# Making the adjacency masks of graphs 2 to 15 on GpSimd instead of VectorE, and waiting for the stored output later

## The chip, the core and the metric

The kernel runs on one core of a Trainium2 chip. A core has five engines that run in parallel, each through its own list of instructions in order, and that wait for each other with semaphores: TensorE (PE; its weight loads are listed as PEld), VectorE (DVE), ScalarE (ACT), GpSimd (POOL) and SyncE (SP), which here only issues DMAs. SBUF is the memory on chip that all of them read and write, PSUM the one that TensorE writes its products to. The metric is the device time of one launch in microseconds (us).

## What is computed

There are 16 graphs of 512 nodes with 256 features. Each goes through two layers of one-head attention and then one layer of eight-head attention, all under the mask that its adjacency matrix gives. Cut to what matters:

```python
mask = adj == 0                                    # adj: (16, 512, 512) int32
for k in range(2):                                 # layers L, of one head
    q = x @ Wq[k].T + bq[k];  kk = x @ Wk[k].T + bk[k]
    scores = where(mask, -1e10, q @ kk.T / SCALE)
    attn = where(mask, 0.0, softmax(scores, axis=2))
    x = layer_norm(x + (attn @ x) @ Wc[k].T, ln_g[k], ln_b[k])
q, k, v = (x @ W + b, split into 8 heads of 32)    # layer H
scores = where(mask, -inf, q @ k.T / sqrt(32))
h = softmax(scores, axis=-1) @ v
out = layer_norm(h @ Wo + bo + x, gamma, beta)
```

## The kernel before

**Tiles and slots.** A tile is 128 rows of one 512x512 score matrix. For each tile TensorE multiplies the scores into a PSUM bank (`ps_s`, three banks), VectorE scales them, adds the mask and takes the row minimum (`masked_s`, line 1017), ScalarE takes the exponential (`probs`, L928), TensorE transposes the result (`ps_t`, L789), and ScalarE copies it to SBUF, or VectorE does for every fourth tile (L934, L1024). Four tiles are a slot: one head (H) of a graph or one layer (L) of it. TensorE makes scores four tiles ahead of the tile that it transposes, and VectorE masks three tiles ahead. With three banks, the scores of tile k+3 need the masking of tile k to be done.

**Loop.** After a prologue, 14 rounds of ten slots (`LOOP_SLOTS`, 40 tiles) run, then a tail. Round i handles heads of graphs i and i+1 and the two one-head layers of graph i+2. The table `LOOP_JOBS` says behind which of the 40 tiles each of the other pieces of work is put, in the lists of all engines that share in it. The names used below: AV is the weighted sum of a one-head layer, N the normalisation of its result `y_l` on VectorE (L1118, it needs `rstd_L` from GpSimd), QK and XW the projections of a one-head layer (`qt`, `kt`, `xw`), QH and V those of the eight-head layer, OG the head outputs, R a reciprocal (L1128), WO the output projection, and M the making of a mask.

**Masks.** Graph b's adjacency comes in two halves of 2 x 128 rows. Both go through the same buffer, `adj_t`, so SyncE issues the load of half 1 (`load_adj`, L449) only when the mask of half 0 has been made. VectorE makes the mask with one instruction for each half, on 128 partitions x 1024 elements, int32 in and bf16 out: (adj == 0) * MASKED (L1069). Half 0 is at `LOOP_JOBS` position 0, half 1 at position 5. The result `mask_a0` serves layer 0 of the graph, and DMAs copy it to `mask_a1` and `mask_h` for the later layers.

**GpSimd's list.** In each round GpSimd copies the residual (`residual`, L677), and then handles two layer norms (`layer_norm_l0`: L622 `rstd_L`, L635 and L637 the split of `y_l` into two fp16 parts `ys`, L627 gain, L629 shift), one split of the next input, and at the end `finish` for graph i: `rstd_F`, four scalings (L684), gain, shift, and the DMA that stores the output (L690). `finish` ends with a wait for that DMA to have landed (`out_stored`), since the residual copy that follows overwrites the same `y_f`.

**The split `ys`** is turned by a DMA transpose (L497) into `xt2`, from which TensorE makes QH some tiles later.

Of the kernel before, what the change touches and what calls it, by code (L numbers as in the profile page):

```python
# [9 lines left out]
NT = N // P  # L10
# [4 lines left out]
MASKED = -1e33  # L15
# [7 lines left out]
LOOPS = NB - 2  # L23
# [7 lines left out]
LOOP_JOBS = [  # L31
    ("AV", (1, 2), "i+1", 1, (0, 0, 1, 1)),
    ("N", None, "i+1", 1, (4,)),
    ("M", None, "i+2", 0, (0,)),
    ("OG", (1, 0), "i", 0, (3, 5, 7)),
    ("R", None, "i", 0, (3,)),
    ("M", None, "i+2", 1, (5,)),
    ("QK", (0, 2), "i+2", 0, (2, 4)),
    ("XW", (2, 0), "i+2", 0, (8, 10)),
    ("QH", (1, 2), "i+1", 0, (12, 13)),  # L40
# [63 lines left out]
def graph_attention(nc, x, adj, l0, l1, out):  # L104
    fp32, fp16, bf16, i32 = mybir.dt.float32, mybir.dt.float16, mybir.dt.bfloat16, mybir.dt.int32
    ALU, ACT = mybir.AluOpType, mybir.ActivationFunctionType
# [6 lines left out]
    with ctx:  # L113
        def sb(name, shape, dt=fp32):
            return ctx.enter_context(nc.sbuf_tensor(name, shape, dt))

        def sem(name):
            return ctx.enter_context(nc.semaphore(name))
# [29 lines left out]
        mask_a0 = sb("mask_a0", [P, NT, N], bf16)  # L148
# [68 lines left out]
        mask0_ready, mask1_ready = sem("mask0_ready"), sem("mask1_ready")  # L217
        maskh_ready = [sem(f"maskh{r}_ready") for r in range(NT)]
        scores_done, masked, exps = sem("scores_done"), sem("masked"), sem("exps")
# [27 lines left out]
        xres_ready, out_stored = sem("xres_ready"), sem("out_stored")  # L247
# [14 lines left out]
        def slots_before(i):  # L262

            return sum(len(slots) for _, slots, _, _ in PRO_BLOCKS) + len(LOOP_SLOTS) * i
# [3 lines left out]
        def nth(b, l):  # L268

            if isinstance(b, int) and b + l == 1:  # L270
                return 2 if l else 1
            return 2 * b + l
# [36 lines left out]
        def x_loaded(b):  # L309

            if early(b, 2):
                return (x_in, 16) if b == 0 else (x1_in, 16)
            return x_in, 16 * b

        def adj_tile(b, h):

            if early(b, 2):
                return (adj_t[:], adj_spare)[h] if b == 0 else adj_next[:, 2 * h:2 * h + 2]
            return adj_t[:]

        def adj_loaded(b, h):

            if early(b, 2):
                return (adj_in, 32) if b == 0 else (adj1_in, 32)
            return adj_in, 16 * (2 * b + h - 1)

        def early(count, n):

            return isinstance(count, int) and count < n

        def settle(eng):


            eng.sem_inc(waits_passed, 1)
# [275 lines left out]
        @blk.gpsimd  # L610
        def _(pool):
            pool.memset(ident[:], 1.0).then_inc(ident_zero, 1)
            pool.memset(minus_half[:], -0.5).then_inc(half_in, 1)
            pool.memset(mean_64[:], 1.0 / 64).then_inc(mean_in, 1)
            pool.wait_ge(ident_zero, 1)
            pool.affine_select(out=ident[:], in_=ident[:], compare_op=ALU.is_equal, fill=0.0, base=0,
                               pattern=[[-1, P]], channel_multiplier=1).then_inc(ident_in, 1)

            def rstd_of(s, c):

                pool.wait_ge(moments_ready[s], c + 1)
                pool.tensor_tensor(rstd[s][:], var_eps[s][:], minus_half[:], ALU.pow).then_inc(rstd_ready[s], 1)  # L622

            def gain_and_shift(s, c, y, norm, dst):
                g = gain[:, norm:norm + 1, :].to_broadcast([P, NT, D])
                h = shift[:, norm:norm + 1, :].to_broadcast([P, NT, D])
                pool.tensor_tensor(dst[:], y[:], g, ALU.mult).then_inc(gained[s], 1)  # L627
                pool.wait_ge(gained[s], c + 1)
                pool.tensor_tensor(dst[:], dst[:], h, ALU.add).then_inc(ln_done[s], 1)  # L629

            def split(src, dst, high, ready, n):


                src = src[:].rearrange("p t (c k) -> p c t k", c=DC)
                pool.tensor_copy(dst[:, 0], src).then_inc(high, 1)  # L635
                pool.wait_ge(high, n + 1)
                pool.tensor_tensor(dst[:, 1], src, dst[:, 0], ALU.subtract).then_inc(ready, 1)  # L637

            def split_x(b):

                pool.wait_ge(*x_loaded(b))
                settle(pool)
                if not early(b, 1):
                    pool.wait_ge(xt_in, 16 * (nth(b - 1, 0) + 1))
                    settle(pool)
                split(x_tile(b), xs, xs_hi, xs_ready, b)

            def split_y(b, l):
                rstd_of("L", nth(b, l))

                pool.wait_ge(normed["L"], nth(b, l) + 1)
                settle(pool)

                if l == 0 and early(b, 2):
                    if b == 1:
                        pool.wait_ge(xt_in, 16 * (nth(0, 1) + 1))
                        settle(pool)
                elif l == 1 and early(b, 1):
                    pool.wait_ge(xt_in, 16 * (nth(1, 1) + 1))
                    settle(pool)  # L660
                else:
                    pool.wait_ge(xt2_in, 16 * b)
                    settle(pool)
                    if l == 1:
                        pool.wait_ge(xt_in, 16 * (nth(b, 1) + 1))
                        settle(pool)
                split(y_l, ys, ys_hi, ys_ready, nth(b, l))

            def layer_norm_l0(b, l, dst):
                split_y(b, l)  # L670
                gain_and_shift("L", nth(b, l), y_l, l, dst)

            def residual(b):

                pool.wait_ge(ln_done["L"], 2 * NB if isinstance(b, int) and b == NB - 1 else 2 * b + 3)
                settle(pool)
                pool.tensor_copy(y_f[:], x2[:]).then_inc(xres_ready, 1)  # L677

            def finish(b):
                rstd_of("F", b)  # L680
                pool.wait_ge(rstd_ready["F"], b + 1)
                settle(pool)
                for t in range(NT):
                    last = pool.tensor_scalar(y_f[:, t], y_f[:, t], minus_mean["F"][:, t:t + 1],  # L684
                                              rstd["F"][:, t:t + 1], ALU.add, ALU.mult)
                last.then_inc(normed["F"], 1)
                pool.wait_ge(normed["F"], b + 1)
                gain_and_shift("F", b, y_f, 2, y_f)
                pool.wait_ge(ln_done["F"], b + 1)
                pool.dma_start(out_v[b], y_f[:]).then_inc(out_stored, 16)  # L690
                pool.wait_ge(out_stored, 16 * (b + 1))

            split_x(0)
            split_x(1)
            pool.wait_ge(weights_in, 16 * N_WEIGHTS_IN)

            pool.tensor_tensor(shift[:, 1], shift[:, 1], bo1, ALU.add).then_inc(bo_added, 1)
            pool.wait_ge(bo_added, 1)
            layer_norm_l0(0, 0, x1)

            split_y(1, 0)
            pool.tensor_tensor(y_f[:], y_l[:], gain[:, 0:1, :].to_broadcast([P, NT, D]), ALU.mult)\
                .then_inc(gained["L"], 1)
            split_x(2)
            pool.wait_ge(y_ready["L"], 2 * nth(0, 1) + 2)
            settle(pool)
            pool.wait_ge(gained["L"], nth(1, 0) + 1)
            pool.tensor_tensor(x1[:], y_f[:], shift[:, 0:1, :].to_broadcast([P, NT, D]), ALU.add)\
                .then_inc(ln_done["L"], 1)
            layer_norm_l0(0, 1, x2)  # L710
            for i in range(LOOPS - 1):
                residual(i)
                layer_norm_l0(i + 1, 1, x2)
                layer_norm_l0(i + 2, 0, x1)
                split_x(i + 3)
                finish(i)
            residual(LOOPS - 1)
            layer_norm_l0(LOOPS, 1, x2)
            layer_norm_l0(LOOPS + 1, 0, x1)
            finish(LOOPS - 1)  # L720
            residual(NB - 2)
            layer_norm_l0(NB - 1, 1, x2)
            finish(NB - 2)
            residual(NB - 1)
            rstd_of("F", NB - 1)
# [275 lines left out]
        def _(dve):  # L1001
# [58 lines left out]

            def make_mask(b, h):

                if h == 0 and not early(b, 1):
                    dve.wait_ge(mask1_ready, 16 * b)
                if early(b, 2) and b == 1:
                    dve.wait_ge(masked, NT)
                dve.wait_ge(*adj_loaded(b, h))
                settle(dve)
                dve.tensor_scalar(mask_a0[:, 2 * h:2 * h + 2], adj_tile(b, h), 0.0, MASKED, ALU.is_equal,  # L1069
                                  ALU.mult).then_inc(mask0_ready, 1)  # L1070
# [194 lines left out]
```

## Time and profile before

| | us |
|---|---|
| median of the three runs shown | 1263.99 |
| lowest, highest | 1263.12, 1269.35 |
| the profiled execution, its own time | 1263.8 |
| its span in the profile | 1262.1 |
| busy: PE, DVE, ACT, POOL | 1168.8, 1046.9, 879.6, 491.5 |
| granted TensorE clock | 0.994 of full speed |

The span is the time from the first to the last recorded instruction; the launch takes 1.7 us more. Each engine's busy time is the time in which it had an instruction in execution. The profile and the trace come from one execution, so every duration below is of that one.

### The profile page before, as it was taken

What the parts mean: (1) busy time and instruction counts of PE and PEld (TensorE: products, weight loads), DVE (VectorE), ACT (ScalarE), POOL (GpSimd) and SP (SyncE); (2) the same over time, 40 slices, a digit from 0 to 9 for tenths busy, and PEclk for the clock granted to TensorE, in tenths of its full rate; (3) what the DMA queues carried; (4) which work ended last, traced back from release to release, by engine and by line L of the source; (5) the groups of instructions that cost most, each with busy time, mean ns of one, the idle gap of its engine ahead of it and who ended that gap; (6) DMA issues with size and microseconds to landing.
All of it is one profiled execution on the core that took longest, in us unless ns stands there. A gap on an engine that the chain in (4) does not pass through costs nothing.

```text
span 1262.1 us, 28364 instructions
## 1 busy us (share of the span) xinstructions
PE 1168.8 (93%) x9440; PEld 843.7 (67%) x9440; DVE 1046.9 (83%) x2771; ACT 879.6 (70%) x2018; POOL 491.5 (39%) x338
## 2 busy tenths in 40 slices
PE   4876999999999999999999999999999999999896
PEld 2643667677676767767676776767677676776564
DVE  3776888979798897979889797988979888897786
ACT  3235786777778677786767778676777867677674
POOL 2342233443363344336333433633344354334420
PEclk9999999999999999999999999999999999999999
DMA  8115263353625234271523527254342724333321
GB/s 251 50 34 137 48 159 76 103 117 92 160 51 163 73 101 118 83 169 51 153 84 100 118 71 182 52 136 100 97 122 69 183 52 138 97 81 89 84 69 34
DMA packets 182208, 130.84 MB, mean 104 GB/s; under 512 B 108464, under 2 KB 161712, under 8 KB 182064
## 3 DMA queue, kind: packets, MB, share of 16 engines
q1 hardware_dynamic: 179904, 121.16, 37.3%
q0 software_dynamic: 2160, 7.87, 1.8%
q8 instruction: 78, 1.28, 0.4%
q14 instruction: 66, 0.54, 0.1%
HBM read 61.87 MB, written 25.17 MB: 69 GB/s over the span
## 4 chain that ended last, share of the span: by engine, by line
PE 52%; DVE 23%; issue 11%; ACT 10%; DMA 2%; SPq 1%; POOL 1%; DVEq 0%; ACTq 0%; POOLq 0%
PE ps_j L776 17%; PE ps_t L789 13%; PE ps_j L877 9%; DVE masked_s L1017 8%; PE ps_s L768 5%; ACT probs L928 4%; PE ps_j L894 4%; PE ps_s L762 3%; DVE y_l L1161 2%; ACT pt_h L934 2%; DVE pt_l L1052 2%; DVE parts L1169 2%; DVE stats_L L1037 2%; ACT parts L973 1%; ACT xw L965 1%
## 5 line engine op out<-in xcount | busy, mean ns | idle before, releaser
L928 ACT ACTIVATE probs<-masked_s,nm_h 128x512 f32<-128x512 f32 x512 | 367.7, 718 | 137.6 <-DVE nm_h L1017 136.5
L789 PE MATMUL ps_t<-ident,probs 128*128 128x128 f32 x2560 | 390.6, 275 | 37.7 <-ACT pt_h L934 20.1
L789 PEld LDWEIGHTS ps_t<-ident,probs 128*128 128x128 f32 x2560 | 301.6, 141 | 132.7 <-ACT probs L928 63.6
L1017 DVE CUSTOM_DVE_ANT_0 masked_s<-ps_s,mask_h 128x512 f32<-128x512 f32 x512 | 341.9, 681 | 54.8 <-PE ps_s L768 54.6
L934 ACT ACTIVATE pt_h<-ps_t 128x512 f32<-128x512 f32 x376 | 221.9, 590 | 93.6 <-PE ps_t L789 90.2
L768 PE MATMUL ps_s<-stack 128*128 128x512 f16 x512 | 194.0, 380 | 9.2 <-DVE nm_h L1017 6.5
L776 PE MATMUL ps_j<-xw,pt_l 128*128 128x256 f16 x1536 | 186.3, 276 | 3.6 <-DVE pt_l L1052 3.6
L776 PEld LDWEIGHTS ps_j<-xw,pt_l 128*128 128x128 f16 x1536 | 151.9, 99 | 32.4 <-DVE pt_l L1052 3.9
L622 POOL TENSOR_TENSOR rstd_L<-var_eps_L,minus_half 128x4 f32<-128x4 f32 x32 | 32.8, 1024 | 301.3 <-DVE var_eps_L L1047 301.3
L877 PE MATMUL ps_j<-pt_h,v 128*32 128x256 f32 x2048 | 123.6, 382 | 1.7 <-DVE pt_h L1024 1.7
L622 POOL TENSOR_TENSOR rstd_F<-var_eps_F,minus_half 128x4 f32<-128x4 f32 x16 | 16.3, 1018 | 275.5 <-DVE var_eps_F L1047 275.5
L776 PE MATMUL ps_j<-xt,wq 128*128 128x512 f16 x384 | 95.7, 386 | 20.1 <-DMA xt<-xs 13.6
L1024 DVE COPY pt_h<-ps_t 128x512 f32<-128x512 f32 x136 | 93.3, 686 | 19.0 <-PE ps_t L789 18.7
L1052 DVE TENSOR_TENSOR pt_l<-ps_t,pt_l 128x512 f16<-128x512 f32 x128 | 88.3, 690 | 19.5 <-ACT pt_l L934 13.4
L928 ACT ACTIVATE probs<-masked_s,nm_l 128x512 f32<-128x512 f32 x128 | 92.1, 720 | 16.2 <-DVE nm_l L1017 16.2
L776 PE MATMUL ps_j<-wc,xt 128*128 128x256 f16 x768 | 97.8, 273 | 5.0 <-DVE qt L1136 5.0
L934 ACT ACTIVATE pt_l<-ps_t 128x512 f16<-128x512 f32 x96 | 56.7, 591 | 62.8 <-PE ps_t L789 62.7
L762 PE MATMUL ps_s<-kt,qt 128*128 128x512 f16 x372 | 99.6, 379 | 0.2
L928 ACT ACTIVATION_READ_ACCUMULATOR probs<-masked_s,nm_h 128x1 f32 x512 | 97.8, 191 | 0.0
L877 PEld LDWEIGHTS ps_j<-pt_h,v 128*32 128x32 f32 x2048 | 60.3, 109 | 53.2 <-issue 19.3
L776 PE MATMUL ps_j<-xt,wk 128*128 128x512 f16 x384 | 94.0, 381 | 0.0
L776 PEld LDWEIGHTS ps_j<-wc,xt 128*128 128x128 f16 x768 | 74.9, 98 | 25.7 <-issue 5.8
(107 smaller groups left out, 1718.9 us busy)
## 6 DMA issues: line engine op xcount, KB each, us to landing
stack<-bounce SPq DMA_DIRECT2D x256, 128.0 KB, 3.2
bounce<-parts SPq DMA_DIRECT2D x64, 256.0 KB, 3.1
adj_t<-adj_dram SPq DMA_DIRECT2D x29, 512.0 KB, 4.7
x<-x_dram SPq DMA_DIRECT2D x16, 512.0 KB, 4.0
mask_a<-mask_a SPq DMA_DIRECT2D x16, 512.0 KB, 4.0
mask_h<-mask_a SPq DMA_DIRECT2D x64, 128.0 KB, 3.3
out_dram<-y_f POOLq DMA_DIRECT2D x15, 512.0 KB, 3.4
stack<-adj_dram SPq DMA_DIRECT2D x2, 512.0 KB, 5.8
```

Source lines behind the costliest of these rows:

```text
L622: pool.tensor_tensor(rstd[s][:], var_eps[s][:], minus_half[:], ALU.pow).then_inc(rstd_ready[s], 1)
L762: last = pe.matmul(dst, q_t[:, a, r * P:(r + 1) * P], k_t[:, c], start=n_ == 0, stop=n_ == 2)
L768: pe.matmul(dst, stack[:, n, 0, r * P:(r + 1) * P], stack[:, n, 1, :], start=True, stop=True).then_inc(scores_done, 1)
L776: last = pe.matmul(dst, lhs(a, e), rhs(c, e), start=n == 0, stop=n == len(terms) - 1 and not more)
L789: last = pe.transpose(ps_t[r % 2][:, t], probs[:, r, t * P:(t + 1) * P], ident[:])
L877: last = pe.matmul(out_bank[h * HD:(h + 1) * HD, 2 * r * P:2 * (r + 1) * P], v1[:, t, col:col + HD], pt_h[:, h, t, 2 * r * P:2 * (r + 1) * P],
L894: last = pe.matmul(out_bank[:, t * D:(t + 1) * D], ot[:, g, at:at + P], wo1[:, g], start=g == 0, stop=g == 1)
L928: act.activation(probs[:, r], masked_s[:, r], ACT.Exp, bias=nm[:, n, r:r + 1], scale=-1.0, accum_out=total[:, n, r:r + 1]).then_inc(exps, 1)
L934: act.activation(dst, ps_t[r % 2][:], ACT.Copy).then_inc(copied_act, 1)
L1017: dve.tensor_tensor_reduce(out=masked_s[:, r], in0=ps_s[scores_bank(pos)][:], in1=m[:, r], scale=-scale, scalar=NONE_LEFT, op0=ALU.add, op ...
L1024: dve.tensor_copy(dst, ps_t[r % 2][:]).then_inc(copied_dve, 1)
L1052: dve.tensor_tensor(dst, full, high, ALU.subtract).then_inc(ready, 1)
```

## The change

The two M entries leave the table of the loop, so VectorE makes masks only for graphs 0 and 1, in the prologue. GpSimd gets a `make_mask` of its own, with the same instruction. It calls it for half 0 ahead of the residual copy of a round, and for half 1 behind that copy and ahead of the layer norm that was next. The wait for the stored output leaves the end of `finish` and stands at the start of the next `residual`, so behind mask half 0.

```diff
@@ LOOP_JOBS
-    ("M", None, "i+2", 0, (0,)),
     ("OG", (1, 0), "i", 0, (3, 5, 7)),
     ("R", None, "i", 0, (3,)),
-    ("M", None, "i+2", 1, (5,)),
@@ gpsimd
+            def make_mask(b, h, passed):
+
+                if h == 0:
+                    pool.wait_ge(mask1_ready, 16 * b)
+                    settle(pool)
+                    pool.wait_ge(masked, passed)
+                    settle(pool)
+                pool.wait_ge(*adj_loaded(b, h))
+                settle(pool)
+                pool.tensor_scalar(mask_a0[:, 2 * h:2 * h + 2], adj_tile(b, h), 0.0, MASKED, ALU.is_equal,
+                                   ALU.mult).then_inc(mask0_ready, 1)
+
             def residual(b):
 
+                if not early(b, 1):
+                    pool.wait_ge(out_stored, 16 * b)
+                    settle(pool)
                 pool.wait_ge(ln_done["L"], 2 * NB if isinstance(b, int) and b == NB - 1 else 2 * b + 3)
@@ finish
                 pool.dma_start(out_v[b], y_f[:]).then_inc(out_stored, 16)
-                pool.wait_ge(out_stored, 16 * (b + 1))
@@ the rounds
             for i in range(LOOPS - 1):
+                make_mask(i + 2, 0, NT * slots_before(i))
                 residual(i)
+                make_mask(i + 2, 1, NT * slots_before(i))
                 layer_norm_l0(i + 1, 1, x2)
                 layer_norm_l0(i + 2, 0, x1)
                 split_x(i + 3)
                 finish(i)
+            make_mask(LOOPS + 1, 0, NT * slots_before(LOOPS - 1))
             residual(LOOPS - 1)
+            make_mask(LOOPS + 1, 1, NT * slots_before(LOOPS - 1))
             layer_norm_l0(LOOPS, 1, x2)
@@ vector
             def make_mask(b, h):
 
-                if h == 0 and not early(b, 1):
-                    dve.wait_ge(mask1_ready, 16 * b)
-                if early(b, 2) and b == 1:
+                if b == 1:
                     dve.wait_ge(masked, NT)
```

GpSimd's list where round 0 ends and round 1 begins, before (`x` and `y_f` are the residual's source and target):

```order
L629 TENSOR_TENSOR y_f<-y_f,shift 128x1024 [waits gained_F]
L690 DMA out_dram<-y_f 128x4x256 [waits ln_done_F]
L677 COPY y_f<-x 128x1024 [waits out_stored,ln_done_L]
L622 TENSOR_TENSOR rstd_L<-var_eps_L,minus_half 128x4 [waits moments_ready_L]
L635 CAST ys<-y_l 128x1024 [waits normed_L,xt2_in,xt_in]
L637 TENSOR_TENSOR ys<-y_l,ys 128x1024 [waits ys_hi]
```

and now:

```order
L627 TENSOR_TENSOR y_f<-y_f,shift 128x1024 [waits gained_F]
L703 DMA out_dram<-y_f 128x4x256 [waits ln_done_F]
L680 TENSOR_SCALAR mask_a<-adj_t 128x1024 [waits mask1_ready,masked,adj_in]
L690 COPY y_f<-x 128x1024 [waits out_stored,ln_done_L]
L680 TENSOR_SCALAR mask_a<-adj_t 128x1024 [waits adj_in]
L620 TENSOR_TENSOR rstd_L<-var_eps_L,minus_half 128x4 [waits moments_ready_L]
L633 CAST ys<-y_l 128x1024 [waits normed_L,xt2_in,xt_in]
```

The two masks stand around the copy, both of them ahead of `rstd_L`.

VectorE's list around mask half 1 in the same round, before (`y_l` L1118 is N, `kt` the low part of the QK projection, the two ISA rows of L1017 the masking of one tile and the reading of its row minimum):

```order
L1017 ISA masked_s,nm_h<-ps_s,mask_h 128x512 [waits scores_done,exps]
L1017 ISA nm_h 128x1
L1118 TENSOR_SCALAR y_l<-y_l,minus_mean_L,rstd_L 128x256 [waits rstd_ready_L]
L1118 TENSOR_SCALAR y_l<-y_l,minus_mean_L,rstd_L 128x256 x3
L1136 SCALAR_TENSOR_TENSOR kt<-ps_j,bk,kt 128x512 [waits qk_hi]
L1017 ISA masked_s,nm_h<-ps_s,mask_h 128x512 [waits scores_done,exps]
L1017 ISA nm_h 128x1
L1069 TENSOR_SCALAR mask_a<-adj_t 128x1024 [waits adj_in]
L1017 ISA masked_s,nm_h<-ps_s,mask_h 128x512 [waits scores_done,exps]
L1017 ISA nm_h 128x1
L1024 COPY pt_h<-ps_t 128x4x128 [waits transposed]
```

and now:

```order
L1033 ISA masked_s,nm_h<-ps_s,mask_h 128x512 [waits scores_done,exps]
L1033 ISA nm_h 128x1
L1132 TENSOR_SCALAR y_l<-y_l,minus_mean_L,rstd_L 128x256 [waits rstd_ready_L]
L1132 TENSOR_SCALAR y_l<-y_l,minus_mean_L,rstd_L 128x256 x3
L1150 SCALAR_TENSOR_TENSOR kt<-ps_j,bk,kt 128x512 [waits qk_hi]
L1033 ISA masked_s,nm_h<-ps_s,mask_h 128x512 [waits scores_done,exps]
L1033 ISA nm_h 128x1
L1033 ISA masked_s,nm_h<-ps_s,mask_h 128x512 [waits scores_done,exps]
L1033 ISA nm_h 128x1
L1040 COPY pt_h<-ps_t 128x4x128 [waits transposed]
```

Only the mask row is gone. Half 0 leaves in the same way, further up in the same round. The lists of TensorE, ScalarE and SyncE are the same in both kernels.

## Rows read from the trace of the kernel before

**Rows 1.** The page, part 1: busy time, share of the span, instructions.

```profile
PE 1168.8 (93%) x9440; PEld 843.7 (67%) x9440; DVE 1046.9 (83%) x2771; ACT 879.6 (70%) x2018; POOL 491.5 (39%) x338
```

**Rows 2.** Busy time by engine in one stretch of 74 us, then clock, DMA share.

```profile
358.00:432.00 74.00, 71.73 (x590) 52.42 (x588) 63.94 (x170) 54.91 (x127) 31.12 (x21) 1.00 0.40 108
```

**Rows 3.** Busy time of line 1069 alone, from the first round to the last.

```profile
137.00:1115.00 978.00, 39.54 (x28) 1.00 0.42 107
```

**Rows 4.** TensorE, 425 to 472 us: start, length, line, work, idle before and releaser.

```profile
427.11 0.63 PE L789 MATMUL ps_t<-ident,probs 128*128 128x128 f32 x4 [0.83 <-DVE pt_l L1052]
...
445.09 0.81 PE L762 MATMUL ps_s<-kt,qt 128*128 128x512 f16 x3
...
452.27 1.46 PE L776 MATMUL ps_j<-xt,wq 128*128 128x512 f16 x6
453.56 0.60 PE L789 MATMUL ps_t<-ident,probs 128*128 128x128 f32 x4
...
470.04 0.39 PE L768 MATMUL ps_s<-stack 128*128 128x512 f16 x1 [0.46 <-DVE nm_h L1017]
471.45 0.63 PE L789 MATMUL ps_t<-ident,probs 128*128 128x128 f32 x4 [1.03 <-ACT pt_h L934]
```

**Rows 5.** VectorE, 432 to 446 us, same columns.

```profile
432.74 0.68 DVE L1069 TENSOR_SCALAR mask_a<-adj_t 128x1024 bf16<-128x1024 int32 x1
...
439.34 0.69 DVE L1017 CUSTOM_DVE_ANT_0 masked_s<-ps_s,mask_h 128x512 f32<-128x512 f32 x1 [0.26 <-PE ps_s L768]
...
439.95 1.38 DVE L1118 TENSOR_SCALAR y_l<-y_l,minus_mean_L,rstd_L 128x256 f32<-128x256 f32 x4
442.10 0.75 DVE L1136 SCALAR_TENSOR_TENSOR kt<-ps_j,bk,kt 128x512 f16<-128x512 f32 x1 [0.77 <-ACT kt L962]
442.77 0.68 DVE L1017 CUSTOM_DVE_ANT_0 masked_s<-ps_s,mask_h 128x512 f32<-128x512 f32 x1
...
443.37 2.13 DVE L1069 TENSOR_SCALAR mask_a<-adj_t 128x1024 bf16<-128x1024 int32 x1
```

**Rows 6.** GpSimd, 430 to 447 us, same columns.

```profile
430.79 0.83 POOL L690 DMA_DIRECT2D out_dram<-y_f  x1 [0.30 <-POOL y_f L629]
434.40 1.03 POOL L677 COPY y_f<-x 128x1024 f32<-128x1024 f32 x1 [2.77 <-DMA out_dram<-y_f]
436.48 1.03 POOL L622 TENSOR_TENSOR rstd_L<-var_eps_L,minus_half 128x4 f32<-128x4 f32 x1 [1.06 <-DVE var_eps_L L1047]
441.69 1.04 POOL L635 CAST ys<-y_l 128x1024 f16<-128x1024 f32 x1 [4.18 <-DVE y_l L1118]
442.81 2.14 POOL L637 TENSOR_TENSOR ys<-y_l,ys 128x1024 f16<-128x1024 f32 x1
```

**Rows 7.** SyncE's issues, 430 to 450 us, same columns.

```profile
433.51 0.40 SPq L449 DMA_DIRECT2D adj_t<-adj_dram  x1
445.18 1.74 SPq L497 DMA_TRANSPOSE xt<-ys  x1
```

**Rows 8.** That load's time from issue to landing: round at 507, then at 432 us.

```profile
adj_t<-adj_dram SPq DMA_DIRECT2D x1, 512.0 KB, 3.6
...
adj_t<-adj_dram SPq DMA_DIRECT2D x1, 512.0 KB, 5.0
```

**Rows 9.** Landing of the transposes by line 497, all 16: least, median, most.

```profile
DMA to landing us min/median/max: 4.2/4.3/5.9
```

**Rows 10.** GpSimd's groups: busy us, mean ns of one, idle before them.

```profile
L684 POOL TENSOR_SCALAR y_f<-y_f,minus_mean_F,rstd_F 128x256 f32<-128x256 f32 x60 | 32.5, 551 | 3.2 <-POOL rstd_F L622 3.2
L616 POOL TENSOR_SCALAR_AFFINE_SELECT ident<-ident 128x128 f32<-128x128 f32 x1 | 0.3, 284 | 0.0
```

**Rows 11.** ScalarE and VectorE, 453 to 456 us: how the next busy run of VectorE begins.

```profile
453.63 0.72 ACT L928 ACTIVATE probs<-masked_s,nm_l 128x512 f32<-128x512 f32 x1 [0.18 <-DVE nm_l L1017]
...
454.35 0.58 ACT L934 ACTIVATE pt_l<-ps_t 128x512 f16<-128x512 f32 x1
...
455.04 0.69 DVE L1052 TENSOR_TENSOR pt_l<-ps_t,pt_l 128x512 f16<-128x512 f32 x1 [0.18 <-ACT pt_l L934]
```

## The prediction

> **What bounds the kernel now.** The page's busy times come first [rows 1]: TensorE works 93% of the span, VectorE 83%, GpSimd 39%. Read by stage, the rounds are tighter still: of 74 us in one round TensorE is busy 71.73 [rows 2], so only 2.27 us in a round are open to any change that leaves TensorE's own work alone, 14 x 2.27 = 32 us in all. The next question is where in the round these 2.27 us lie. TensorE's timeline shows idle time in two places only: before 427.11 (0.83 us), and before 470.04 and 471.45 (0.46 and 1.03 us), the rest being crumbs [rows 4]. Each time the releaser is VectorE or ScalarE behind it. Between 427.7 and 469 TensorE's instructions follow each other without a wait. Both masks of the round, at 432.74 and 443.37 [rows 5], lie in that stretch. So VectorE's time there isn't what the round's length is made of.
>
> **What is removed.** 28 mask instructions leave VectorE, with 39.54 us together [rows 3], 2.8 us in a round: 0.68 us for half 0, 2.13 us for half 1 [rows 5]. It is the same instruction; the second starts at 443.37 while GpSimd's subtraction of `ys` runs from 442.81 to 444.95 [rows 6], and 444.95 + 0.55 is the 445.50 at which it ends. What the 39.54 us are worth on the path: in the stretch of the masks TensorE has no wait to lose, so nothing there. Of the gain something gets through only if VectorE enters its next full stretch earlier, the one at whose end the two idle times at 470 and 471 lie. That stretch begins at 455.04 with a statement that waited 0.18 us for ScalarE's copy of 454.35, which came late because ScalarE's exponential had waited 0.18 us for a masking at 453.63 [rows 11]. The copy can't start before its transposes, 453.56 with 0.60 us [rows 4], are through at 454.16 and have been signalled. So an earlier VectorE moves the start of the full stretch by 454.35 - 454.2 = 0.15 us, no more. 13 to 14 rounds x 0.15 = 2 us faster.
>
> The Trainium skill, "SBUF — State Buffer", section "Who interferes with whom", says that VectorE's two-port instructions and GpSimd's hold the shared ports exclusively, and that the later one blocks in full. The 2.13 us against 0.68 agree with it. By that rule alone 1.45 us of each round's 2.8 was blocking and would be gained too; by the timeline it is hidden like the rest.
>
> **What is added: GpSimd's two masks.** Their length D has no row. The nearest from below is a one-input copy of the same 1024 elements, 1.03 us [rows 6]. From above: the scaling with two operations takes 0.551 us for 256 elements, four of which are 2.2; the one instruction with a comparison, 0.284 us for 128, would give 8 x 0.284 = 2.3 [rows 10]. Fixed costs are counted four and eight times in these, so the value lies between the ends; I take D = 1.8, and keep 1.0 to 2.3 as likely, with more as a rival.
>
> The Trainium skill, "GPSIMD Engine Reference", section "Engine selection", says that one-input operations on GpSimd run at roughly line rate. The copy's row agrees, the scaling's row does not, and the mask is of the scaling's kind. With D = 1.0 by the page the sum below would be the same 2 us.
>
> **Half 0** costs nothing: the DMA issue ends at 430.79 + 0.83 = 431.6, and GpSimd then waited 2.77 us, to 434.40, for the stored output [rows 6]. The mask fills that wait (431.7 to 433.5 with D = 1.8), which is what moving `out_stored` behind it allows. Its other conditions are met: VectorE's own mask at 432.74 started without a wait for the adjacency [rows 5], and VectorE masks three tiles ahead, so the round's last tile is masked well before its end. The cover is gone at D above 2.7.
>
> **Half 1** is the dear one, since it stands ahead of `rstd_L`, on which VectorE's N waits with everything behind it. With L the landing time of the load: half 0 ends at 431.7 + D, SyncE issues 0.1 later (433.51 after 433.42 before), the data are there L later, the mask takes D, `rstd_L` 1.03 and the semaphores between 0.25. N can start at 431.8 + D + L + D + 1.3 = 433.1 + L + 2D. It started at 439.95, right after a masking that TensorE had held [rows 5], so the missing half 0 mask doesn't bring it forward. The delay is S = L + 2D - 6.85. L is 3.6 us in the round at 507 and 5.0 in the one at 432 [rows 8]; of the 14 rounds nine are within 0.1 us of the first value, and the other five go up to the second. With D = 1.8 S is 0.35 us with the short load and 1.75 with the long one.
>
> Who waits for that? Behind N stand `kt` and the masking of 442.77 [rows 5]. TensorE needs both at 445.09 [rows 4] (`kt` directly, and the masking because it frees the bank). From N's start the three take 1.33 + 0.67 + 0.68 = 2.7 us (1.38, 0.75, 0.68 in their rows, of which the first two overlap the next a little), and must be done by 445.0: N may start at 442.3, so S may be 2.35. After that masking VectorE saves the 2.13 us of half 1, so every later statement is earlier than before. The other follower is the split `ys`, which moves with N; its transpose was issued at 445.18 [rows 7] and lands 4.3 us later [rows 9], at 449.5, and TensorE's QH begins at 452.27 [rows 4]: 2.8 us of slack. Both hold for S = 1.75. Half 1's cost: 0, as long as L + 2D < 9.2, that is D < 2.8 with the short load and D < 2.1 with the long one. At the upper end, D = 2.3, three or four rounds with the long load lose 0.4 us, less than 2 us in all. The prologue and the tail keep their lists.
>
> **The sum.** 1263.8 (the profiled run) - 2 + 0 = 1261.8; against the median 1263.99 it is the same within 0.2 us. I forecast 1262.
>
> **The rivals.**
>
> *GpSimd's mask is slow, and half 1 holds VectorE (slower).* For: no row shows a comparison on 1024 int32 elements, and GpSimd's power of 4 elements takes 1.03 us [rows 6], so some operations there are far from the copy's rate. It decides from D = 2.8. Beyond it each of 13 rounds loses S - 2.35 = L + 2D - 9.2, with L = 4.0 on average 2D - 5.2: at D = 3.0 0.8 us, 10 us together and 1272; at D = 4.0 2.8 us, 36 us and 1298. Against: the three nearest rows give 1.0 to 2.3. Chance 0.18, most of it near the threshold, with the price at D = 3.0 as its own forecast.
>
> *VectorE's relief comes through (faster).* VectorE has 2.8 us less in each round, and if its backlog instead of the order of arrival makes the idle times at 470 and 471, they close: 14 x 1.49 = 21 us, 1243; a third of it is 1257. For: VectorE is the releaser, and runs without idle time before it. Against: it waits for ScalarE at 455.04 [rows 11], between the masks and that stretch, so that the gained time is given back there. Chance 0.12.
>
> *The change doesn't fill a wait.* Half 1 is not in the 2.77 us but in the 4.18 us that GpSimd waited for N [rows 6], which itself waits for what GpSimd has to do first. This is the first rival at smaller D, and costs nothing below the threshold; its chance of 0.1 is inside that of no change.
>
> **How the numbers follow.** What a measurement of this kernel can tell from no change is about 0.5%, 6.3 us. Hidden, as summed: 0.70. Slower: 0.18. Faster: 0.12. The forecast's own spread is 1258 to 1268. The range goes down to 1253, past the third of the relief, and up to 1275, past the D = 3.0 case; outside remain some 0.08 on the slow side and 0.07 on the fast side.
>
> **What would show it.** VectorE's busy time falls by about 39 us and GpSimd's rises by 28 x D, near 50. `out_dram`'s wait before the residual copy shrinks from 2.77 us to about 0.9. GpSimd's idle time before half 1 is charged to the load `adj_t`. VectorE gets a wait of 0.3 to 1.8 us on `rstd_L` before N in each round, and TensorE has none in that stretch. Its idle times at 427, 470 and 471 stay, the last two shorter by 0.15. A mask longer than 2.8 us on GpSimd, or an idle TensorE before the scores that use `kt`, would make the forecast wrong upward; the idle time at 470 gone would make it wrong downward.

## The result and the profile after

| | before | after |
|---|---|---|
| median, four runs each | 1265.77 | 1286.32 |
| lowest, highest | 1263.12, 1269.35 | 1283.1, 1288.03 |
| the profiled execution, and its span | 1263.8, 1262.1 | 1286.17, 1284.4 |

The changed kernel is slower: the ratio is 1.0158, with a 95% interval of 1.0122 to 1.0193. The forecast was 1262 us, 2 us below the kernel before, with a range of 1253 to 1275. The measured time lies above the range, and the change went the other way.

Part 1 of the page of after, which answers to [rows 1], gives busy time, share of the span and instructions:

```profile
PE 1181.2 (92%) x9440; PEld 850.0 (66%) x9440; DVE 1012.7 (79%) x2743; ACT 882.4 (69%) x2018; POOL 586.4 (46%) x366
```

VectorE lost 34 us of work and GpSimd gained 95, on a span that is 22.3 us longer. What GpSimd gained is named by its groups (part 5 of the page: busy us, mean ns of one, idle time before them and what ended it):

```profile
L680 POOL TENSOR_SCALAR mask_a<-adj_t 128x1024 bf16<-128x1024 int32 x28 | 102.2, 3650 | 68.9 <-DMA adj_t<-adj_dram 41.9 <-DVE nm_h L1033 26.5
```

One mask takes 3.65 us on GpSimd. The forecast had put 1.8 on it, from rows of 1.0 to 2.3 us [rows 10].

The round at 511 us shows what this does. First GpSimd, 505 to 535 us (start, length, line, work, idle before and releaser), which answers to [rows 6]:

```profile
510.14 0.87 POOL L703 DMA_DIRECT2D out_dram<-y_f  x1 [0.30 <-POOL y_f L627]
511.05 3.67 POOL L680 TENSOR_SCALAR mask_a<-adj_t 128x1024 bf16<-128x1024 int32 x1
514.66 1.04 POOL L690 COPY y_f<-x 128x1024 f32<-128x1024 f32 x1
518.77 3.63 POOL L680 TENSOR_SCALAR mask_a<-adj_t 128x1024 bf16<-128x1024 int32 x1 [3.06 <-DMA adj_t<-adj_dram]
522.37 1.04 POOL L620 TENSOR_TENSOR rstd_L<-var_eps_L,minus_half 128x4 f32<-128x4 f32 x1
525.19 1.04 POOL L633 CAST ys<-y_l 128x1024 f16<-128x1024 f32 x1 [1.78 <-DVE y_l L1132]
```

SyncE issues the load of half 1 behind the first mask, and it lands 3.8 us later (SyncE's timeline, and the DMA issues of that stretch, which answer to [rows 7] and [rows 8]):

```profile
514.83 0.40 SPq L447 DMA_DIRECT2D adj_t<-adj_dram  x1
```

```profile
adj_t<-adj_dram SPq DMA_DIRECT2D x1, 512.0 KB, 3.8
```

VectorE in the same round, which answers to [rows 5]:

```profile
515.72 0.16 DVE L1063 TENSOR_SCALAR var_eps_L<-moments_L 128x4 f32<-128x4 f32 x1
...
518.86 0.69 DVE L1033 CUSTOM_DVE_ANT_0 masked_s<-ps_s,mask_h 128x512 f32<-128x512 f32 x1 [0.30 <-PE ps_s L784]
...
523.44 1.38 DVE L1132 TENSOR_SCALAR y_l<-y_l,minus_mean_L,rstd_L 128x256 f32<-128x256 f32 x4 [3.88 <-POOL rstd_L L620]
524.74 0.75 DVE L1150 SCALAR_TENSOR_TENSOR kt<-ps_j,bk,kt 128x512 f16<-128x512 f32 x1
525.40 0.68 DVE L1033 CUSTOM_DVE_ANT_0 masked_s<-ps_s,mask_h 128x512 f32<-128x512 f32 x1
```

And TensorE, which answers to [rows 4]:

```profile
524.19 0.60 PE L805 MATMUL ps_t<-ident,probs 128*128 128x128 f32 x4
526.15 0.82 PE L778 MATMUL ps_s<-kt,qt 128*128 128x512 f16 x3 [1.36 <-DVE nm_h L1033]
```

Read the four together. The input of `rstd_L`, `var_eps_L`, is there at 515.9 us. But `rstd_L` stands in GpSimd's list behind mask half 1, whose data land at 518.6, so it starts at 522.37. N on VectorE waits 3.88 us for it. The masking behind N therefore ends at 526.1, and TensorE, whose next scores need that bank and `kt`, stands still for 1.36 us. Before, the scores that use `kt` began without a wait, in the round at 432 us [rows 4] as in the one at 507 us, which is the round shown here:

```profile
519.35 0.81 PE L762 MATMUL ps_s<-kt,qt 128*128 128x512 f16 x3
```

How often TensorE waits like this is in the views of waits of after, over the whole span (waiting line, released by: us in total, times, longest). TensorE:

```profile
PE ps_s L778 <- DVE nm_h L1033: 16.7, 13, 1.6
```

GpSimd and VectorE:

```profile
POOL mask_a L680 <- DMA adj_t<-adj_dram: 41.9, 14, 3.1
```

```profile
DVE y_l L1132 <- POOL rstd_L L620: 52.4, 17, 4.1
```

So 16.7 of the 22.3 us are this wait, 13 times, 0.8 to 1.6 us each. Of the rest, 3.4 us are in the tail, where the one long wait for a transpose of `ys` is 3.18 us (2.35 before) and the granted clock then drops. In the windows of after (us, busy time and instructions of PE, PEld, DVE, ACT, POOL, then clock, DMA share, GB/s) it is 0.83 over 20 us, where the same work before had 1.00 throughout:

```profile
1205.00:1215.00 10.00, 8.74 (x41) 5.00 (x42) 3.85 (x11) 4.80 (x10) 0.62 (x1) 0.83 0.10 37
1215.00:1225.00 10.00, 7.81 (x44) 5.46 (x42) 7.20 (x20) 9.52 (x25) 0.00 (x0) 0.83 0.79 227
```

Another 1.7 us are in two late rounds, in which TensorE waits 0.61 and 0.42 us for a transpose of `ys`. That transpose comes later because N does: it is issued 2.5 us behind the start of the scores that use `kt` in almost every round, against 0.1 us before. In these two rounds it also landed late, 5.4 and 5.2 us after its issue where 4.3 is usual. Such a landing alone did no harm before (5.9 us in two rounds, no wait), and the later issue alone does none in the others; the two together use up the 2.8 us of slack that the prediction had found. Round 0 is a control inside the run: there GpSimd had its first mask made by 131.8, half 1 started at 135.81, N at 144.08 waited for nothing, and TensorE had no such wait.

### The profile page after: what moved, and what is told of

It is laid out like the page before. It is cut to its first block, busy times and chain, and to the rows that moved or that the text cites. A ratio compares the mean times of both kernels' runs of the same rounds, so it can differ in the third digit from the quotient of the medians.

```text
span 1284.4 us, 28406 instructions
## 1 busy us (share of the span) xinstructions
PE 1181.2 (92%) x9440; PEld 850.0 (66%) x9440; DVE 1012.7 (79%) x2743; ACT 882.4 (69%) x2018; POOL 586.4 (46%) x366
## 3 DMA queue, kind: packets, MB, share of 16 engines
q8 instruction: 78, 1.28, 0.4%
## 4 chain that ended last, share of the span: by engine, by line
PE 41%; DVE 21%; POOL 17%; issue 8%; DMA 6%; ACT 6%; SPq 1%; DVEq 0%; POOLq 0%; ACTq 0%
PE ps_j L792 12%; PE ps_t L805 11%; POOL mask_a L680 7%; PE ps_j L893 6%; DVE masked_s L1033 5%; PE ps_s L778 5%; PE ps_j L910 4%; DMA adj_t<-adj_dram 3%; PE ps_s L784 3%; ACT probs L944 2%; POOL y_f L625 2%; POOL y_f L627 2%; DVE y_l L1175 2%; POOL y_f L697 2%; DVE parts L1183 2%
## 5 line engine op out<-in xcount | busy, mean ns | idle before, releaser
L805 PEld LDWEIGHTS ps_t<-ident,probs 128*128 128x128 f32 x2560 | 305.0, 142 | 130.2 <-ACT probs L944 59.8
L680 POOL TENSOR_SCALAR mask_a<-adj_t 128x1024 bf16<-128x1024 int32 x28 | 102.2, 3650 | 68.9 <-DMA adj_t<-adj_dram 41.9
L778 PE MATMUL ps_s<-kt,qt 128*128 128x512 f16 x372 | 100.3, 382 | 16.8 <-DVE nm_h L1033 16.7
L792 PE MATMUL ps_j<-xt,wk 128*128 128x512 f16 x384 | 96.9, 390 | 0.0
```

What stands on the lines that cost most here:

```text
L680: pool.tensor_scalar(mask_a0[:, 2 * h:2 * h + 2], adj_tile(b, h), 0.0, MASKED, ALU.is_equal, ALU.mult).then_inc(mask0_ready, 1)
L778: last = pe.matmul(dst, q_t[:, a, r * P:(r + 1) * P], k_t[:, c], start=n_ == 0, stop=n_ == 2)
L792: last = pe.matmul(dst, lhs(a, e), rhs(c, e), start=n == 0, stop=n == len(terms) - 1 and not more)
L805: last = pe.transpose(ps_t[r % 2][:, t], probs[:, r, t * P:(t + 1) * P], ident[:])
```

## The experiments

Theory **A**: the mask of 3.65 us, twice in a chain with the load between them and ahead of `rstd_L`, holds N. Rival **B**: GpSimd's longer work gets in the way of VectorE's by itself, wherever it stands. Rival **C**: it is the later wait for the stored output. Each median below stands beside that of the kernel before on the same chip, over 10 runs of the experiment's kernel where nothing else is said. The ratio on record, with its 95% interval, isn't the quotient of the two medians and can differ from it by 0.1%; the verdicts go by the ratio.

**1. Mask half 1 behind the split of `ys`.** Same masks, same lengths; only `rstd_L` and the split go first. This tells A from B.

```diff
-            def layer_norm_l0(b, l, dst):
+            def layer_norm_l0(b, l, dst, masks=None):
                 split_y(b, l)
+                if masks is not None:
+                    make_mask(masks, 1, 0)
...
-                make_mask(i + 2, 1, NT * slots_before(i))
-                layer_norm_l0(i + 1, 1, x2)
+                layer_norm_l0(i + 1, 1, x2, masks=i + 2)
...
```

> The changed kernel with one thing moved: GpSimd makes mask half 1 behind the split of y_l into ys, no longer ahead of rstd_L. Theory A (VectorE's N waits for rstd_L behind mask half 1, 3.65 us each, and TensorE then waits 1.2 to 1.5 us a round for the masking behind N): the 3.9 us wait before N and TensorE's wait go, 1264 +-3. Theory B (GpSimd's 102 us of masks slow the other engines wherever they run, by the shared port or by memory): the masks are still there, so about the changed kernel's time, 1283 to 1289. Theory C (half 1 here ends too late for the first use of the mask, some 3.7 us behind): about 1270, with a wait of VectorE on the mask.

Measured: 1263.65 beside 1265.86, ratio 0.9988 (0.9972 to 1.0004). The whole loss is gone. GpSimd's timeline of this kernel:

```profile
510.17 1.04 POOL L620 TENSOR_TENSOR rstd_L<-var_eps_L,minus_half 128x4 f32<-128x4 f32 x1 [0.27 <-DVE var_eps_L L1063]
...
518.65 3.65 POOL L682 TENSOR_SCALAR mask_a<-adj_t 128x1024 bf16<-128x1024 int32 x1
```

The mask is as long as ever, so B falls. (The theory C of this expectation isn't the rival C above; it says that half 1 comes too late for its first use.) VectorE now waits for the mask itself, a few tiles later, and its waits of the whole span say so:

```profile
DVE masked_s L1033 <- POOL mask_a L682: 21.7, 14, 1.9
```

In the rounds TensorE has no wait behind that (the scores that use `kt` wait nowhere), so the expectation's theory C costs nothing either. A wait of VectorE costs time only where it outlasts what TensorE can spare behind it.

**2 and 3. One half alone.** Half 0 goes back to VectorE (2, with its old wait for `mask1_ready`), or half 1 does (3).

```diff
@@ 2
+    ("M", None, "i+2", 0, (0,)),
...
-                make_mask(i + 2, 0, NT * slots_before(i))
                 residual(i)
...
@@ 3
+    ("M", None, "i+2", 1, (5,)),
...
                 residual(i)
-                make_mask(i + 2, 1, NT * slots_before(i))
...
```

> Half 0 back on VectorE, half 1 on GpSimd where the change has it. Theory A: the load for half 1 starts when VectorE's half 0 is done, not 3.7 us after GpSimd's DMA issue; N can start at 433.4 + 3.6 + 3.65 + 1.3 = 442.0 by the clock of the round shown of before, 2.1 us late, under the 2.35 us that TensorE tolerates: VectorE waits 2 us for rstd_L in each round, TensorE waits not at all, 1264 +-4. Theory B: half of GpSimd's masks, half of the loss, about 1275.

> Half 0 on GpSimd where the change has it, half 1 back on VectorE. Theory A: half 0 (3.65 us) ends 1 us after the stored output has landed, the residual copy is 1 us late and rstd_L hardly; the load of half 1 lands some 4 us before VectorE's half 1: 1264 +-3. Theory B: half of the loss, about 1275.

Measured: half 1 alone 1270.53 beside 1265.86, ratio 1.0026 (1.001 to 1.0041); half 0 alone 1265.56, ratio 0.9995 (0.9982 to 1.0008). With half 1 alone, D counts once. In the round of an ordinary load N waits 2.10 us:

```profile
517.94 1.38 DVE L1133 TENSOR_SCALAR y_l<-y_l,minus_mean_L,rstd_L 128x256 f32<-128x256 f32 x4 [2.10 <-POOL rstd_L L621]
```

TensorE stands still only in the four rounds with a slow load (its waits, 300 to 1100 us):

```profile
PE ps_s L777 <- DVE nm_h L1032: 3.4, 4, 1.5
```

The forecast for 2 was 1264 +-4 with no wait of TensorE, and the median is 2.5 us above that. It had counted on the short load. In the four rounds that wait, the load took 4.2 to 5.6 us, in the others 3.6 to 3.8. This is the threshold of the prediction, met from both sides. The two halves aren't additive: alone they cost 3 us (5 by the medians) and 0 us, together 20. What half 0 adds is a later load of half 1. SyncE issues it 3.82 us behind the end of GpSimd's DMA issue in the changed kernel (514.83 against 511.01) and 2.05 us behind it in 2 (509.35 against 507.30). The difference of 1.77 us is that of N's waits, 3.88 against 2.10.

**4. The same values by add and multiply.** The adjacency is 0 or 1, so (adj - 1) * (-MASKED) gives the same mask.

```diff
-                pool.tensor_scalar(mask_a0[:, 2 * h:2 * h + 2], adj_tile(b, h), 0.0, MASKED, ALU.is_equal,
+                pool.tensor_scalar(mask_a0[:, 2 * h:2 * h + 2], adj_tile(b, h), -1.0, -MASKED, ALU.add,
```

> The changed kernel with the mask computed as (adj - 1) * 1e33, the same values for an adjacency of 0 and 1, so add and multiply in place of comparison and multiply; same sizes, types and places. If the comparison makes the 3.65 us, the mask takes what the scalings of 4 x 256 elements suggest, about 2.2 us, N can start 2.9 us earlier, which is more than TensorE's wait of 1.3: 1264 +-4. If the 1024 int32 elements make it, 3.6 us and 1286. In between each us of the mask's length is worth 2 us a round down to the threshold, so at 3.0 us the loss is gone.

Measured: 1267.1 beside 1265.86, ratio 0.9999 (0.9985 to 1.0012). The loss is gone here too, with the list of the changed kernel untouched. The mask's line in this kernel (ns: least, median, most), and then in the changed one:

```profile
L680 POOL TENSOR_SCALAR mask_a<-adj_t x28: 1045/1046/1059, 127.6 to 1100.7; 128x1024 bf16<-128x1024 int32 x28
```

```profile
L680 POOL TENSOR_SCALAR mask_a<-adj_t x28: 3627/3644/3685, 128.1 to 1122.9; 128x1024 bf16<-128x1024 int32 x28
```

The same tile, types and number of operations: it is the comparison that costs 2.6 us. The length was expected at 2.2 us and is half of that.

**5. Mask half 1 made twice.** The longer chain, on the other side of the threshold.

```diff
...
+                if h == 1:
+                    pool.tensor_scalar(mask_h2[:], adj_tile(b, h), 0.0, MASKED, ALU.is_equal, ALU.mult)
                 pool.tensor_scalar(mask_a0[:, 2 * h:2 * h + 2], adj_tile(b, h), 0.0, MASKED, ALU.is_equal,
```

> The changed kernel, with GpSimd computing mask half 1 twice in a row (first into a spare buffer), so 3.63 us more between the load and rstd_L in each round. Theory A, TensorE waiting 1:1 for what is behind N: 13 rounds x 3.63 = 47 us on top of the changed kernel, 1333 +-6, and VectorE's wait before N 7.5 us. If something else makes the loss and N's wait only accompanies it, the time rises by less than half of that, under 1310.

Measured, two runs: 1362.22 beside 1266.38, ratio 1.0758 (1.0736 to 1.0779). The direction is A's, but the size is a miss: 76 us over the changed kernel instead of 47. TensorE in one round:

```profile
554.64 1.46 PE L781 MATMUL ps_s<-kt,qt 128*128 128x512 f16 x3 [4.91 <-DVE nm_h L1036]
...
560.69 0.81 PE L781 MATMUL ps_s<-kt,qt 128*128 128x512 f16 x3
```

The wait grew from 1.36 to 4.91 us, by 3.55, as the added 3.6 us ask for. But the three matmuls behind it take 1.46 us and not 0.81. The windows (columns as above) show why:

```profile
555.00:560.00 5.00, 5.00 (x21) 3.27 (x20) 2.70 (x8) 3.25 (x9) 4.92 (x3) 0.51 0.29 56
560.00:565.00 5.00, 5.00 (x36) 3.63 (x35) 3.62 (x8) 4.54 (x11) 1.68 (x1) 1.00 0.27 50
```

TensorE stood still for 4.9 us, and in the 5 us behind that wait it was granted 0.51 of full speed, the lower of its two levels, so it did some 2.4 us less work in them. From the first of these waits to the last the rounds take 81.3 us on average, against 75.5 in the changed kernel. Of these 5.8 us the waits make 3.6 (4.88 against 1.28 on average), and 2.2 are left for the low clock, which every one of the 13 rounds had. 13 x 5.8 is the 76 us.

**6. A buffer of its own for half 1.** The load of half 1 no longer waits for mask half 0; the masks keep their length and place.

```diff
...
+        adj_u = sb("adj_u", [P, NT // 2, N], i32)
...
-            return adj_t[:]
+            return (adj_t, adj_u)[h][:]
...
-            return adj_in, 16 * (2 * b + h - 1)
+            return (adj_u_in, 16 * (b - 1)) if h else (adj_in, 16 * (b + 1))
...
-                    sp.wait_ge(mask0_ready, 2 * b + h)
+                    sp.wait_ge(mask0_ready, 2 * b)
```

> The changed kernel with a second adjacency buffer, so that the load of half 1 no longer waits for mask half 0: the 3 us of the load leave the chain, both masks keep their 3.65 us and their places. Theory A: from the start of half 0 to N there are 3.65 + 1.04 + 3.65 + 1.3 = 9.6 us instead of 12.4; TensorE tolerates 11.0 (12.4 less its wait of 1.36), so it doesn't wait, 1264 +-4, with about 1 us of wait left on VectorE before N. If the masks' own length ahead of rstd_L were enough for the loss, 1275 or more.

Measured: 1266.56 beside 1266.38, ratio 1.0004 (0.9993 to 1.0015). GpSimd, then VectorE, in one round (its first mask starts at 507.12):

```profile
511.75 3.63 POOL L682 TENSOR_SCALAR mask_a<-adj_u 128x1024 bf16<-128x1024 int32 x1
```

```profile
516.42 1.38 DVE L1134 TENSOR_SCALAR y_l<-y_l,minus_mean_L,rstd_L 128x256 f32<-128x256 f32 x4 [0.34 <-POOL rstd_L L622]
```

N starts 9.3 us after the first mask instead of 12.4, inside what TensorE tolerates, and the scores that use `kt` wait in no round. VectorE's wait before N is 0.34 us, where about 1 us was expected. So the loss has three conditions, and taking any one away is enough: the mask's length (4), the load in series between the masks (6), and the place ahead of `rstd_L` (1).

**7. The moved wait alone.** The kernel before, with `out_stored` waited for at the next residual.

```diff
+                if not early(b, 1):
+                    pool.wait_ge(out_stored, 16 * b)
+                    settle(pool)
...
-                pool.wait_ge(out_stored, 16 * (b + 1))
```

> The kernel before with only the wait for the stored output moved to the start of the next residual copy; the masks stay on VectorE. Nothing stands between the old and the new place of the wait in the rounds, so nothing can change but where it is booked: 1264 +-3, the same as before. If the moved wait had a part in the loss, it is slower.

Measured: 1265.63 beside 1265.8, ratio 1.0005 (0.9991 to 1.002). C falls.

**8 to 11. Is VectorE's time worth anything?** With the loss gone, kernels 1, 4 and 6 still give nothing for the work that VectorE no longer has. The prediction's faster rival said that the idle times at 470 and 471 are VectorE's backlog. So in 8 the layer-0 N, which lies right in VectorE's full stretch, goes from the kernel before to GpSimd, and in 9 from kernel 4:

```diff
-    ("N", None, "i+2", 0, (18,)),
...
+                    for t in range(NT):
+                        last = pool.tensor_scalar(y_l[:, t], y_l[:, t], minus_mean["L"][:, t:t + 1],
+                                                  rstd["L"][:, t:t + 1], ALU.add, ALU.mult)
```

> The kernel before, masks on VectorE as there, but the normalisation of layer 0 (N, four instructions, 1.35 us of VectorE in the full stretch that ends at TensorE's idle times at 470 and 471) done by GpSimd, which sits idle there. If the stretch in which VectorE is full sets those idle times (0.46 + 1.03 us), taking 1.35 us out of it shortens every round by 1.2 to 1.4 us: 1246 to 1250. If ScalarE or the transposes set them, nothing: 1262 to 1266. It tells whether VectorE's time is worth anything, and where.

> The changed kernel with the add and multiply mask (1.05 us) and with layer 0's normalisation on GpSimd. If VectorE's masks are hidden before as the timeline says, this is the same as the normalisation alone on the kernel before, within 0.3%: the masks add nothing to it, 1244 to 1250.

Measured: 8 gives 1266.09 beside 1266.38, ratio 1.0001 (0.9985 to 1.0016), which is the expectation's second branch, nothing gained. 9 gives 1265.12, ratio 0.9991 (0.9978 to 1.0004): the same as 8, as expected, but not the 1244 to 1250. The two idle times of 0.46 and 1.03 us became one of the same sum (TensorE of 8):

```profile
472.62 0.63 PE L795 MATMUL ps_t<-ident,probs 128*128 128x128 f32 x4 [1.50 <-ACT pt_h L940]
```

Its releaser is ScalarE, which has two copies of the QH projection ahead of the exponential and the copy that TensorE waits for (ScalarE of 8, same stretch):

```profile
470.03 0.68 ACT L979 ACTIVATE parts<-ps_j,bq 128x512 f16<-128x512 f32 x1
...
471.17 0.73 ACT L934 ACTIVATE probs<-masked_s,nm_h 128x512 f32<-128x512 f32 x1
471.87 0.60 ACT L940 ACTIVATE pt_h<-ps_t 128x512 f32<-128x512 f32 x1
```

So 10 takes kernel 4 and puts the second of the two QH pieces two tiles later, and 11 adds the N on GpSimd:

```diff
-    ("QH", (2, 0), "i+1", 1, (19, 19)),
+    ("QH", (2, 0), "i+1", 1, (19, 21)),
```

> The changed kernel with the add and multiply mask, and the second half of QH (c = 1) two tiles later in all lists (19 and 21, not 19 and 19). TensorE's idle 1.03 us at the equivalent of 471.45 ends with a copy that ScalarE makes behind both QH parts (468.71 to 470.0) and an exponential. If ScalarE's list sets that idle time, taking 0.6 us out from ahead of the copy and giving TensorE 1.3 us of matmuls among bare transposes shortens each round by 0.5 to 1.2 us: 1248 to 1258. If VectorE's N does (it stays here), 1262 to 1266.

> As g2, and layer 0's normalisation on GpSimd besides. If both VectorE's full stretch and ScalarE's list stand behind the same idle time, each alone gives little and the two together give most of the 1.49 us of a round: 1244 to 1250, and clearly below g2. If ScalarE's list is all, the same as g2.

Measured: 10 gives 1271.85 (four runs) beside 1265.8, ratio 1.0052 (1.0035 to 1.0068), and 11 gives 1266.36, ratio 1.0006 (0.9993 to 1.0019). Both are misses. Kernel 10 is slower, and no run here isolates why: in its profiled run the rounds are only 0.25 us longer each (74.23 against 73.98 on average). In 11 the idle time sits elsewhere again, behind VectorE:

```profile
468.11 0.63 PE L811 MATMUL ps_t<-ident,probs 128*128 128x128 f32 x4 [1.02 <-DVE pt_h L1046]
```

Neither VectorE's time (8, 9) nor ScalarE's order (10) removes this idle time, and the two together (11) don't either. What would remove it stays open, and no kernel here beats the one before by more than the measurement can tell.

## Why the prediction was wrong

**The step that failed is D**, the length of the mask on GpSimd: taken as 1.8 us, its likely upper end 2.3, measured 3.65. No row before showed a comparison on this many elements, and the upper ends were read from other operations: an arithmetic scaling, and one comparison of another kind on 128 elements [rows 10]. The scaling's rows misled the other way for plain arithmetic. Scaling up from 256 elements gave 2.2 us, and the add and multiply on 1024 took 1.05 (experiment 4). The scaling also reads its two scalars from SBUF and the mask has them as constants, and no run here tells what of the difference that makes. So neither row was a guide to the operation beside it, and the step's argument that D must lie between the ends of such rows doesn't hold.

**The structure around D held.** The working puts N 1.4 + L + 2D behind the start of the first mask. With L = 3.8 and D = 3.65 this is 12.5 us; the trace has 523.44 - 511.05 = 12.39. Experiment 6 takes L and the wait for it out, 9.6 forecast and 9.3 measured. In experiment 2 half 0's D is out of the chain, and N's wait falls to 2.10 us.

**The slower rival came true, smaller than its formula.** L + 2D - 9.2 is 1.9 us per round; the trace has 1.36. The tolerance was computed as 442.3 - 431.7 = 10.6 us from the start of the mask. It was 12.39 - 1.36 = 11.0: TensorE reached these scores at 524.79, 13.7 us behind the mask's start and not 13.4 [rows 4], and N came 0.1 us earlier than 12.5. The two make 0.45 of the 0.5 us of difference. Half of the 0.3 us is no effect of the change: from the end of GpSimd's DMA issue to these scores it is 13.47 us in the round at 432 of before, 13.65 in the one at 507 and 13.78 in the changed kernel. The rival's average over the rounds was too high for another reason too. It took L = 4.0, since five loads of half 1 took 3.8 to 5.0 us before; in the 13 rounds of the changed kernel that wait, all take 3.6 to 3.8 us. With L = 3.7 the formula gives 1.8 us a round, 23 us, where the waits sum to 16.7. Why the long loads are gone isn't shown; each of them is issued later in its round. The rival's chance, 0.18, was too small for a case that turned on one number that no row showed.

**Half 0 at no cost: right for half 0 alone, but not for the reason given.** Kernel 3 measures it. The cover was gone, as D is above 2.7: the copy at 514.66 follows the mask without idle time, not with the 0.9 us that was forecast. It costs nothing there, since `rstd_L` has no input before 515.9, which the prediction hadn't counted on. With half 1 on GpSimd as well, half 0 does cost, by way of the load.

**Next to nothing gained from VectorE's 39.5 us: right.** VectorE's busy time fell by 34 us and not by 39: each mask's row overlaps its neighbours by 0.08 us at either end, which stays busy without it (28 x 0.16 = 4.5 us). The idle time that answers to 470 shrank by 0.05 us on average, less than the 0.15 allowed, as the views of waits of before and of after say:

```profile
PE ps_s L768 <- DVE nm_h L1017: 6.5, 16, 0.5
```

```profile
PE ps_s L784 <- DVE nm_h L1033: 5.7, 16, 0.5
```

The idle time that answers to 471 stayed at 1.03 us. The forecast gain of 2 us, 0.16%, is less than the intervals can show; kernels 1, 3, 4 and 6 leave no room for a gain above 0.3%. Kernel 8 makes this stronger than the prediction had it: even VectorE's time inside its full stretch is worth nothing alone.

**The signs to look for** told the cases apart. GpSimd's busy time rose by 95 us, not near 50. The idle time before half 1 is charged to the load (3.06 us), as forecast. N's wait is 3.88 us, not 0.3 to 1.8. TensorE waits before the scores that use `kt`, which the prediction had named as what would make it wrong upward.

## What to carry to other kernels

When an instruction moves to another engine, its length there is that of this very operation: a comparison isn't an addition. Where no row shows it, write down from which length the neighbours lose, and if that lies within a factor of two of the guess, the losing case deserves a chance near even. An instruction put into an in-order list ahead of one that others wait for brings its own waits along (here a load behind another mask, so that the mask's length counts twice); put behind that one, the same 3.65 us were free. And a wait of 4 us on an engine next to the bound costs only what exceeds the slack of whoever follows.

## What the runs showed of the hardware

- On GpSimd, comparing and multiplying 128 x 1024 int32 into bf16 takes 3.65 us; adding and multiplying the same tile takes 1.05 us. VectorE makes the compared one in 0.68 us, or in 2.13 us where GpSimd's subtraction of `ys` runs beside it [rows 5, rows 6].
- The scaling of 256 elements on GpSimd takes 0.55 us [rows 10] and the arithmetic mask of 1024 takes 1.05, four times the elements in twice the time. The two differ in the source of their scalars and in their types as well.
- TensorE's granted clock was 0.51 in the 5 us behind 4.9 us without work in experiment 5, which had such a low stretch in each of 13 rounds, at some 2 us a round. After the wait of 1.36 us in the changed kernel it stayed at 1.00 (the window behind it, columns as above):

```profile
526.00:531.00 5.00, 4.85 (x36) 3.62 (x37) 3.89 (x12) 4.88 (x13) 4.84 (x4) 1.00 0.17 35
```
